# A two-layer graph network on one core: the per-group dense step moved to three groups at a time, two accumulators, and the adjacency built in flat sets of eight windows

## The reference

```python
def _mp_layer(x, src, dst, edge_attr, W, b):
    loops = jnp.arange(n); src2 = cat[src, loops]; dst2 = cat[dst, loops]; ea2 = cat[edge_attr, 0]
    msg = jnp.concatenate([x[dst2], x[src2], ea2], axis=1) @ W + b
    return jax.nn.relu(jax.ops.segment_sum(msg, dst2, num_segments=n))
h   = relu(_mp_layer(x, src, dst, edge_attr, W1, b1))      # 64 -> 128
out = log_softmax(_mp_layer(h, src, dst, edge_attr, W2, b2), axis=1)   # 128 -> 64
x   = _layernorm(x + out)
```

## Time and profile before

| | us |
|---|---|
| median of 3 runs | 244.36 (244.24 to 245.3) |
| the profiled execution, its own time | 245.42 |
| its span in the profile | 243.6 |
| busy: PE / DVE / ACT / POOL | 203.7 / 179.0 / 118.6 / 148.1 |
| PE L874, layer 1, 625 matmuls | 74.2 |
| PE L849, build, 600 matmuls | 59.0 |
| PE L882, layer 2, 625 matmuls | 52.8 |
| ACT L762, copies to adj, 75 | 77.5 |

### The profile page before, as it was taken

How to read it: one execution, slowest core, us unless ns; L and a number is a source line. 1 busy time by engine, 2 the same in 40 slices (tenths; PEclk the granted TensorE clock), 3 DMA queues, 4 the chain that set the end, 5 groups by cost and what they waited for, 6 DMA issues and landing times.

```text
span 243.6 us, 5581 instructions
## 1 busy us (share of the span) xinstructions
PE 203.7 (84%) x2092; PEld 182.0 (75%) x2092; DVE 179.0 (73%) x459; ACT 118.6 (49%) x242; POOL 148.1 (61%) x334
## 2 busy tenths in 40 slices
PE   0423498999989999899998999989999999999940
PEld 0113497888768798778987789878889999999930
DVE  2968989887876978889788897777201193998982
ACT  2406466667557677576775767757720010111110
POOL 6549351899977999978999689999674000000000
PEclk9999999999979999999999999999999999999995
DMA  1340100000000000000000000000000001011000
GB/s 40 110 125 0 44 0 3 1 14 2 13 0 13 0 5 0 3 0 4 1 3 0 3 0 6 0 3 1 0 3 3 0 3 32 3 32 25 18 16 17
DMA packets 8908, 3.31 MB, mean 14 GB/s; under 512 B 8091, under 2 KB 8406, under 8 KB 8881
## 3 DMA queue, kind: packets, MB, share of 16 engines
q1 hardware_dynamic: 7841, 1.98, 4.0%
q0 software_dynamic: 1040, 0.97, 1.6%
HBM read 2.13 MB, written 0.81 MB: 12 GB/s over the span
## 4 chain that ended last, share of the span: by engine, by line
PE 40%; POOL 27%; DVE 19%; DMA 6%; issue 4%; ACT 1%; DVEq 0%; POOLq 0%; ACTq 0%
PE pset L882 21%; PE acc L874 9%; DVE ohr L530 5%; PE pset L849 5%; DVE ohl L530 5%; POOL u L381 4%; POOL deg L380 3%; POOL u L384 3%; DMA x_nat<-in_x_tiles 2%; POOL t L399 2%; DMA adj<-in_edges,adj 2%; POOL adj L324 2%; POOL zr L397 2%; POOL t L395 2%; DVE s_sum L561 2%
## 5 line engine op out<-in xcount | busy, mean ns | idle before, releaser
L762 ACT ACTIVATE adj<-pset 125x1000 bf16<-125x1000 f32 x75 | 77.5, 1033 | 10.7 <-PE pset L849 10.7
L874 PE MATMUL acc<-x,adj 125*125 125x195 bf16 x625 | 74.2, 256 | 1.5 <-DVE s_sum L561 1.4
L530 DVE TENSOR_TENSOR ohl<-iota,keys 128x1000 bf16<-128x1000 bf16 (+1 forms) x75 | 56.8, 758 | 15.3 <-PE dense L862 13.9
L849 PE MATMUL pset<-ohr,ohl 128*125 128x125 bf16 x600 | 59.0, 252 | 9.0 <-DVE ohr L530 8.9
L874 PEld LDWEIGHTS acc<-x,adj 125*125 125x125 bf16 x625 | 58.2, 140 | 5.3 <-issue 1.8
L849 PEld LDWEIGHTS pset<-ohr,ohl 128*125 128x125 bf16 x600 | 50.0, 152 | 11.0 <-DVE ohr L530 6.7
L530 DVE TENSOR_TENSOR ohr<-iota,keys 128x1000 bf16<-128x1000 bf16 (+1 forms) x75 | 57.2, 762 | 0.0
L882 PE MATMUL pset<-z,adj 125*125 125x192 bf16 x625 | 52.8, 246 | 0.0
L882 PEld LDWEIGHTS pset<-z,adj 125*125 125x125 bf16 x625 | 51.7, 136 | 0.3
L380 POOL TENSOR_SCALAR deg<-s_sum 125x1 f32<-125x1 f32 x25 | 12.4, 497 | 18.5 <-DVE s_sum L561 18.5
L561 DVE TENSOR_REDUCE s_sum<-acc 125x65 f32<-125x195 f32 x25 | 9.0, 360 | 17.7 <-PE acc L874 16.3
(11 more groups left out here) (118 smaller groups left out, 255.0 us busy)
## 6 DMA issues: line engine op xcount, KB each, us to landing
x_nat<-in_x_tiles SPq DMA_DIRECT2D x1, 406.2 KB
x_nat<-in_x_tiles SPq DMA_DIRECT2D x1, 375.0 KB
out<-x SPq DMA_DIRECT2D x2, 187.5 KB
out<-x SPq DMA_DIRECT2D x3, 93.8 KB
adj<-in_dst SPq DMA_DIRECT2D x1, 208.5 KB
out<-x SPq DMA_DIRECT2D x1, 125.0 KB
adj<-in_edges,adj POOLq DMA_INDIRECT x5, 4.6
adj<-in_edge_attr,adj POOLq DMA_INDIRECT x5, 3.5
```

Source lines behind the costliest of these rows:

```text
L530: ins = dve.tensor_tensor(out=oh[s][:, :, :, :], in0=iota2[:, 0:Q, :].unsqueeze(1).broadcast_to([128, n, Q, 2]), in1=key[:, g, k0:k0 + 2 * ...
L762: act.activation(adj4[0:Q, g, :, w0:w0 + 8 * WD].rearrange("p h (b e) -> p b h e", b=2), pset[s][0:Q, :, 0:4 * WD * G].rearrange("p b (h e ...
L849: ins = pe.matmul(pset[s][0:Q, i // 4, 0:4 * WD * G].rearrange("p (h e) -> p h e", h=G)[:, :, i % 4 * WD:(i % 4 + 1) * WD], ohl[s][:, i // ...
L874: ins = pe.matmul(acc[0:Q, 0:XW], adj4[0:Q, g, h, :], x3[:, h, :], start=(h == 0), stop=(h == G - 1))
```

## The change

1. *Build.* The windows are numbered 0 to 624 through all groups and built in 79 flat sets of eight (the last has one). `pset` has two buffers of two banks; the one-hot buffers are three. In PSUM a window has its own 128 columns, so a matmul writes 125 neighbouring columns, and ScalarE's copy reads runs of 5; a set that lies across two groups is copied in two instructions. One semaphore each counts one-hots, built sets and copied sets. TensorE's loop is over sets (blocks) b: it builds set b+4 and then does the layer-1 matmuls of the windows of block b.
2. *Two accumulators.* `acc` has two banks, used in turn by the groups. VectorE reads group g after the one-hots of set last_set(g)+8.
3. *Epilogues* of three groups at a time, eight of them (groups 0 to 23), with two banks `epb`: each GpSimd instruction handles 3x64 numbers, the first weights are applied to 375 columns at once, and the three steps on TensorE stand at the ends of three successive blocks, from `turn_block(i)` on.
4. The *last group's epilogue* (group 24) has its elementwise part on VectorE, and TensorE fills its waits with the layer-2 matmuls of groups 0 to 5 on the source groups 0 to 20.
5. GpSimd issues all gathers at the start. The key work of block j and the attribute sums are tied to set numbers (`KEY_BLOCK`, `SUM_SET`).

```diff
+WINDOWS = G * G
+SET = 8
+NSETS = -(-WINDOWS // SET)
+EP = 3
+EPILOGUES = tuple((a, min(a + EP, G)) for a in range(0, G, EP))
+LEAD = 4
+KEY_BLOCK = {1: 5, 2: 18, 3: 36, 4: 46}
+def last_set(g):
+    return (g * G + G - 1) // SET
+def turn_block(i):
+    return -(-EPILOGUES[i][1] * G // SET) + 2
...
-        pset = [pb(f"pset{s}", [128, 2, 512], FP32) for s in range(3)]
-        acc = pb("acc", [128, 512], FP32)
-        dense = pb("dense", [128, 512], FP32)
+        pset = [pb(f"pset{s}", [128, 2, 512], FP32) for s in range(2)]
+        acc = [pb(f"acc{s}", [128, 512], FP32) for s in range(2)]
+        epb = pb("epb", [128, 2, 512], FP32)
... GpSimd
+            for i, (a, b) in enumerate(EPILOGUES[:-1]):
+                gp.wait_ge(acc_read, b)
...
+                gp.tensor_tensor(u[:, 0:n, 0:C], s_sum[:, 0:n, 0:C], x_nat[:, a:b, :], ALU.add).then_inc(sums_read, 1)
...
+                gp.tensor_tensor(u[:, 0:n, C:2 * C], x_nat[:, a:b, :], deg_n.broadcast_to(wide), ALU.mult).then_inc(u_ready, 1)
... VectorE
+            for k in range(4, NSETS):
+                onehots(k)          # waits for built >= k - 2
...
+                for g in range(G):
+                    if k == last_set(g) + 8:
+                        reduce_sums(g)
... ScalarE
+                    ins = act.activation(adj4[0:Q, g, :, i * WD:(i + n) * WD].rearrange("p h (w e) -> p h w e", e=WD),
+                                         rows[:, w - k * SET:w - k * SET + n, 0:WD * G].rearrange("p w (h e) -> p h w e", h=G),
+                                         ACT.Copy)
... TensorE
+            def build(k):
+                if k >= 2:
+                    pe.wait_ge(evac, k - 1)
+                pe.wait_ge(oh_ready, k + 1)
+                for i in range(set_size(k)):
+                    ins = pe.matmul(pset[k % 2][0:Q, i // 4, i % 4 * 128:i % 4 * 128 + WD * G],
+                                    ohl[k % 3][:, i // 2, :, i % 2], ohr[k % 3][:, i // 2, :, i % 2], start=True, stop=True)
             def layer1(g, h0, h1):
                 if h0 == 0:
-                    pe.wait_ge(evac[2], g + 1)
+                    pe.wait_ge(evac, last_set(g) + 1)
-                    if g >= 1:
-                        pe.wait_ge(acc_read, g)
+                    if g >= 2:
+                        pe.wait_ge(acc_read, g - 1)
...
+            for k in range(LEAD):
+                build(k)
+            for b in range(NSETS):
+                if b + LEAD < NSETS:
+                    build(b + LEAD)
...                                  # layer1 of block b's windows
+                for i in range(len(EPILOGUES)):
+                    if b == turn_block(i):
+                        turn_sums(i)      # waits for u_ready >= i + 1
+                    if b == turn_block(i) + 1:
+                        hidden(i)
+                    if b == turn_block(i) + 2:
+                        messages(i)
```

More of the change, by code:

```diff
@@ L330, in _ @@
             gather_attrs(1)
-            gather_edges(2)
-            for s in xnat_in:
-                gp.wait_ge(s, 16)
+            for j in range(2, J):
+                gather_edges(j)
+            for j in range(2, J):
+                gather_attrs(j)
             def split_sums(j):
@@ new lines, in _ @@
+                for g in range(G):
+                    if k == last_set(g) + 8:
+                        reduce_sums(g)
+            for g in range(G):
+                if last_set(g) + 8 >= NSETS:
+                    reduce_sums(g)
+            last = len(EPILOGUES) - 1
+            a = G - 1
+            deg_1 = deg[:, a:G].broadcast_to([Q, C])
+            dve.wait_ge(acc_read, G)
+            dve.tensor_scalar(deg[:, a:G], s_sum[:, 0, C:XC], 1.0, None, ALU.add).then_inc(lchain, 1)
+            dve.tensor_tensor(u_last[:, 0:C], s_sum[:, 0, 0:C], x_nat[:, a, :], ALU.add)
@@ L792, in _ @@
+            last = len(EPILOGUES) - 1
+            copy_z(last - 1)
+            copy_turned(last)
+            copy_hidden(last)
+            copy_z(last)
             na = 0
@@ L841, in _ @@
-            pe.transpose(acc[:, Q:2 * Q], key_f[:, 0, :], ident[0:Q, 0:Q]).then_inc(keyt_done, 1)
-            def build(g, s):
-                if g >= 1:
-                    pe.wait_ge(evac[s], g)
-                pe.wait_ge(oh_ready[s], g + 1)
-                for i in range(8):
-                    ins = pe.matmul(
-                        pset[s][0:Q, i // 4, 0:4 * WD * G].rearrange("p (h e) -> p h e", h=G)[:, :, i % 4 * WD:(i % 4 + 1) * WD],
-                        ohl[s][:, i // 2, :, i % 2], ohr[s][:, i // 2, :, i % 2], start=True, stop=True)
-                ins.then_inc(built[s], 1)
@@ new lines, in _ @@
+            last = len(EPILOGUES) - 1
+            known = EPILOGUES[last - 1][0]
+            pe.wait_ge(z3_ready, last - 1)
+            layer2(0, 0, known)
+            messages(last - 1)
+            layer2(1, 0, known)
+            layer2(2, 0, known)
+            turn_sums(last)
+            layer2(3, 0, known)
+            hidden(last)
+            pe.wait_ge(acc_read, G)
+            layer2(4, 0, known)
+            messages(last)
+            layer2(5, 0, known)
+            pe.wait_ge(z3_ready, last)
@@ L965, in _ @@
+            pe.wait_ge(z3_last_ready, 1)
+            for g in range(6):
+                layer2(g, known, G)
+            for g in range(6, G):
+                pe.wait_ge(acc2_read, g - 5)
                 layer2(g, 0, G)
@@ L967, in _ @@
                     pe.wait_ge(deg_ready, 1)
[L968 to L969 removed]
+                    pe.wait_ge(zs_ready, last + 1)
+                    pe.matmul(epb[0:1, 0, 0:1], deg_sum[:, :], ones_f[:, :], start=True, stop=True).then_inc(degs_ready, 1)
             pe.wait_ge(flag_ready, 1)
```

480 lines of the change are left out of this document (234 added, 246 removed).

## The result

The changed kernel takes 255.78 us (median of 6 runs, 249.95 to 256.8) against 245.06 of the kernel before (6 runs, 244.24 to 245.53, timed with it). The ratio is 1.0275, with a 95% interval of 1.0217 to 1.0334; it counts only the two quickest runs of the changed kernel (249.95 and 253.54), since the four others lie more than 1.5% above the quickest. 229.5 was predicted, and the chance of "slower" was put at 0.11. The profiled execution took 249.95 us, with a span of 248.1 at a mean granted clock of 0.95; in the five others the clock was 0.919 to 0.937, so most executions lose more to it than the profile shows.

A forecast was written before the change was run, and what follows sets the result against it. PE's work and waits were taken as the bound: start 28.2, work 172.9, waits 5.8, clock 1.8, turns 9.0, last epilogue 1.5, tail 9.6 give a 228.8 us span; 229.5 predicted, 8-in-10 range 219 to 242.

The forecast's parts named there:

- The slow clock: Half-speed stretch of PE's clock after the wait before the first turn, counted once: 1.8 us.
- PE's own work: Builds, layer 1, epilogues, keys, slow start and layer 2 on PE: 172.9 us.
- Start: Moment when PE can build set 4: 28.2 us, bounds 27 and 30.
- Builds: 593 build matmuls with contiguous outputs at 0.065 us each: 38.5 us; bounds 0.0575 and 0.070 each.
- Epilogues on PE: PE's three steps, 3.0 us per three groups instead of 4.2; 25.4 us in all, bounds 22 and 35.
- Rival E: No less PE work, epilogues 4.2 per three groups and builds at 0.070: about the time before, 242; chance 0.05.
- rival C: ScalarE becomes the bound, its copy of a full set 1.33 us from reading runs of five: 235; chance 0.12.
- Waits up to the first epilogue: VectorE sets the pace until PE turns the first sums at 51.6 us; PE waits 5.8 us.
- Waits at the next six epilogues: PE waits at each turn for `u`, taken 1.5 us each, bounds 0 and 3.0: 9.0 us.
- rival B: GpSimd's larger instructions stretch in proportion beside VectorE, the four to `u` taking 3.2 not 2.2 us: 237; chance 0.10.
- the last epilogue's waits: PE waits 0.95 for ScalarE's copies and perhaps 0.5 in the last group's steps: 1.5 us.
- rival A: Six turn hand-overs cost 3 us each and PE's clock falls behind each: 249.3, slower than before; chance 0.10.

The follow-up runs named there:

- Experiment 1: Changed kernel with VectorE's reduction of each group two sets earlier (last_set(g)+6, not +8): 233.7 us, ratio 0.9514 to the kernel before.
- experiment 5: Kernel of experiment 4 with build outputs again in PSUM runs of five columns; adjacency wrong, so its 14212 us say nothing; eight builds take 0.58 us.
- Experiment 6: Changed kernel with GpSimd's copy of the degrees into `stats` moved behind the product that completes `u`: 250.21 us, ratio 1.0153 to the kernel before.
- Experiment 3: Changed kernel with 30 unread matmuls on TensorE ahead of its wait for `u` at the first seven turns: 244.96 us, ratio 0.9967.
- experiment 2: Changed kernel with the epilogue steps of groups 0 to 20 two blocks later, reductions unmoved: 237.2 us, ratio 0.9638 to the kernel before.
- experiment 4: Changed kernel with reductions two sets earlier and epilogue steps one block later: 229.54 us, ratio 0.935 to the kernel before.
- experiment 10: Kernel of experiment 4 with one short GpSimd tensor_scalar as soon as the second group's sums are read: 229.0 us, ratio 0.933.

## Why the prediction was wrong

Three steps failed, all in PE's way from the first turn on. The waits at the six later turns were put at 9.0 us and were 13.8. The wait in front of layer 1 for a free accumulator had no term and was 9.7, 6.9 of it in this part. The slow clock was counted once, 1.8, and cost 8.5 in the profiled execution. Experiment 1 takes most of all three away by moving the reductions alone. PE's own work came out as summed.

*What bounds.* The view that the chain leaves GpSimd was right (27% to 8%, though GpSimd is busy 97.4 us and not near 80), and so was the place: what is late next is the hand-over at the turn.

*Start.* 28.2 was taken for the build of set 4; it starts at 27.16, and the first layer-1 matmul at 28.05. It is 1.0 early, inside 27 to 30 and of no weight.

*Builds.* 0.065 taken, 0.060 measured (41.24 to 41.72), and 0.0675 in the blocks of the epilogues (94.94 to 95.48); the lower half of the bounds was the right one for most, and the contiguous output is a reason, as experiment 5 shows. *Epilogues on PE.* Three groups take 0.73 at the turn, 1.00 (93.94 to 94.94) and 1.06 (96.17 to 97.23) at full clock: 2.8 against 3.0. Rival E is refuted, and so is rival C: a copy of a full set is 1.02 us, and PE's builds wait 0.2 us for ScalarE's `adj`. Layer 1 and layer 2 came as summed, and the tail is 10.0 us against 9.6.

*Waits up to the first epilogue.* The first turn was put at 51.6 and came at 51.70, by two errors that cancel. VectorE reached the third reduction sooner than 49.4 (it ends at 48.0), 1.0 of it by the earlier start, and GpSimd's chain took 3.4 us instead of 2.2 because its first instruction stood for 2.25 us. That the first turn was met is luck.

*Waits at the next six epilogues.* 9.0 taken, 13.8 measured (2.36, 2.30, 2.56, 1.54, 2.39, 2.65), inside the bounds and well off the value. I had worked out "1 us late" with VectorE three sets ahead and 3 us with one ahead, and then took the nearest long wait of the old trace, which was of another hand-over. The trace says which of the two cases holds. At the second turn (block 21) PE builds set 25, and the sums of group 5 stand behind the one-hots of set 26:

```profile
67.42 0.64 PE L929 MATMUL pset<-ohr,ohl 128*125 128x125 bf16 x8
67.77 0.67 DVE L563 TENSOR_TENSOR ohr<-iota,keys 128x1000 bf16<-128x1000 bf16 x1
68.57 0.35 DVE L576 TENSOR_REDUCE s_sum<-acc 125x65 f32<-125x195 f32 x1
```

VectorE is one set ahead here, and so it is at the other turns but the fifth; there it is two ahead, and the wait is the shortest, 1.54. It is idle with its buffers full while PE stands at a turn and works on an epilogue, and has lost that lead when the next turn comes. The prediction named that loss and did not draw the conclusion.

GpSimd's chain was too short in the sum as well. At the seventh turn the four instructions up to `u` take

```profile
164.37 0.58 POOL L420 TENSOR_SCALAR deg<-s_sum 125x3 f32<-125x3 f32 x1 [2.08 <-DVE s_sum L576]
164.92 0.96 POOL L421 TENSOR_TENSOR u<-s_sum,x_nat 125x192 f32<-125x192 f32 x1
165.83 0.64 POOL L423 CAST stats<-deg 125x9 bf16<-125x9 f32 x1
166.44 0.94 POOL L424 TENSOR_TENSOR u<-x_nat,deg 125x192 f32<-125x192 f32 x1
```

3.0 us (1.4 alone, at 179.19), near the 3.2 of rival B and not 2.2. It is 3.0 at four of the six turns and 2.6 at two, 4.1 us in sum over the 2.2 of the prediction. Experiment 6 shows that 0.6 us of this chain are 0.6 us of the wait at five turns. How the 4.8 us missing from the term divide between the chain and the lead is not shown, since the 1.5 was not worked out from either.

*A wait left out.* With two accumulators, layer 1 of group g may not start before VectorE has read group g - 2. The reduction stands behind the one-hots of the eighth set after the group's last, and with VectorE hardly ahead of PE it comes late. That was in the code and I had no term for it. It cost 9.7 us, 2.8 of them before the first turn, where they lie inside the 5.8 counted, and 6.9 behind it. Experiment 1 takes them all away.

*The clock.* 1.8 taken, once; 8.5 in the profiled execution. The old trace showed one wait above 1.5 us and one fall behind it; with six more waits put at 1.5 I still counted one fall. Experiment 3 prices the falls at the turns at 7.5 us.

*The sum.* From the first turn to the last matmul the prediction has 167.6 us and the trace 186.4 (51.70 to 238.11): 18.8 more. Turns 4.8, layer 1's waits 6.9, clock 6.7, one-hots 0.8, the last epilogue's waits 0.8 less (0.70 against 1.5): 18.4, and 0.4 is left over, in PE's own work. With 0.4 more of tail and 0.1 at the first turn that is the 19.3 between the spans, 248.1 and 228.8.

So rival A is the nearest to what happened, in place and mechanism, with some of B's stretching. A had "3 us each and the clock falls behind each, 249.3", and the profiled execution took 249.95; but the waits at its six turns were 2.3 us and the falls behind them three, and the waits for accumulators made up the rest, so that its number fits is luck. Its point of decision, 2.3 us per turn, was met (13.8 / 6), the condition that the clock falls each time was not. What spoke against it in the prediction, "a full lead of three sets", was not there: at the turns the lead was one set.

Still open: what decides whether the clock falls. In the changed kernel it fell behind a wait of 1.94 us and not behind ones of 2.30 and 2.39; in experiment 2 it fell behind the last turn's wait of 1.52 and not behind the first's of 1.94. Open too is what holds GpSimd's first instructions.

## What to carry to other kernels

Where the order is written out by hand, the place of a piece of work in an engine's queue says how far ahead the engine must be for it to be on time. Here the sums stood one set of one-hots beyond what TensorE was building when it needed them, which asks for a lead that VectorE did not keep. Put what another engine waits for (a reduction that frees an accumulator, sums that start an epilogue) by the smallest lead that a trace shows, not by the number of buffers. Two sets' difference in one place of the order was worth 18.6 us, where the whole change lost 6.7. When steps are merged to make fewer hand-overs, ask what each wait then does to TensorE's clock: in the changed kernel a fall cost 1.7 us behind a wait of 1.9 to 3.0, and the waits of up to 1.12 us at the turns of experiment 4 cost nothing but themselves.

## What the runs showed that I had not expected

GpSimd beside VectorE's one-hots does not slow by a factor. At the seventh turn instructions of 3 and 9 numbers take 0.58 and 0.64 us and those of 192 take 0.96 and 0.94, where alone they take 0.23 and 0.20, and 0.57 and 0.51. The short ones last about as long as the one-hot beside them (0.59 from start to start), the long ones as one that is itself drawn out. Both engines are slowed:

```profile
165.38 1.04 DVE L563 TENSOR_TENSOR ohl<-iota,keys 128x1000 bf16<-128x1000 bf16 x1
166.34 0.67 DVE L563 TENSOR_TENSOR ohr<-iota,keys 128x1000 bf16<-128x1000 bf16 x1
```

A one-hot of 0.59 takes 0.96 (165.38 to 166.34) while GpSimd works on 192 numbers. The Trainium skill, "GPSIMD Engine Reference", section "8. Key points", says that the two share their SBUF interfaces and that VectorE instructions with two SBUF inputs contend. The trace agrees, in that each is drawn out beside the other; no run here isolates the interfaces as the reason.

GpSimd's first instructions of the stage, beside a VectorE that did not pause, took 2.25 to 6.48 us for two or three numbers per partition. Most came after 7.9 to 15.2 us of rest, but the second one of experiment 10 (3.68 us) after 0.54, so the rest alone does not explain them. In the kernel before, whose GpSimd was at work just ahead of it, the same step took 0.66.

Eight builds of 125 columns take 0.48 us with a contiguous PSUM output and 0.55 to 0.58 in runs of five. The Trainium skill, "TensorE: Matmul & The Clock Gate", section "Back-to-back issue gap", has about 81 ns for a pair of weight load and matmul at 128 columns, set by both of them and not by the weight load alone, as the prediction put it. The trace does not agree: 60 ns are measured here at 125 columns.
